# Best-32 attention: turned groups and the exponent's bias shared with VectorE, and a shorter exact path

## The reference, cut to what matters

```
scores = einsum('bthd,bghd->bhtg', Q, K) / sqrt(32)      # 2 batches, 4 heads, 256 x 4096
topv, topi = lax.top_k(scores, 32)
probs = softmax(topv)                                    # zero for all other keys
attn_mean = attn.mean(axis=heads)
c_t = einsum('btg,bgd->btd', attn_mean, x_vision) @ Wv
```

## Time and profile before

| what | value |
|---|---|
| median of three runs | 1144.29 us |
| the three runs | 1147.24, 1140.45, 1144.29 us |
| the profiled execution | 1140.79 us, its span 1139.5 us |
| busy in the span: TensorE | 955.4 us (84%) |
| VectorE | 848.7 us (74%) |
| ScalarE | 651.4 us (57%) |
| GpSimd | 295.7 us (26%) |

### The profile page before, as it was taken

The page is one execution under the profiler, slowest core; times in us unless marked ns, Lnnn a source line. Parts: engine busy times, 40 slices in busy tenths (PEclk is TensorE's granted clock), DMA queues, the critical chain, the costliest instruction groups (busy, mean ns, idle before and its releaser), DMA issues. The chain is left out here.

```text
span 1139.5 us, 20829 instructions
## 1 busy us (share of the span) xinstructions
PE 955.4 (84%) x7631; PEld 599.1 (53%) x7648; DVE 848.7 (74%) x1772; ACT 651.4 (57%) x1067; POOL 295.7 (26%) x313
## 2 busy tenths in 40 slices
PE   5997859999999999996989989248878888987586
PEld 5876724444444444443668875134555556634354
DVE  5775789999899999942567876998878785265447
ACT  3442307788788888874445425059999997202121
POOL 1000088899600000000112521006373631000010
PEclk9999958999999999997789996567799989997797
DMA  5867642222222222200312228002363136830000
GB/s 178 310 234 272 239 134 61 76 79 83 76 74 79 81 79 77 74 1 12 103 49 77 71 61 221 1 1 60 97 181 87 56 98 209 203 110 1 1 1 19
DMA packets 99322, 111.83 MB, mean 98 GB/s; under 512 B 26658, under 2 KB 75731, under 8 KB 99219
## 3 DMA queue, kind: packets, MB, share of 16 engines
q1 hardware_dynamic: 96802, 109.50, 32.0%
q10 hardware_dynamic: 2416, 0.99, 0.4%
HBM read 80.95 MB, written 29.43 MB: 97 GB/s over the span
## 5 line engine op out<-in xcount | busy, mean ns | idle before, releaser
L835 ACT ACTIVATE pT<-bank 128x512 f32<-128x512 f32 x512 | 278.5, 597 | 93.2 <-PE bank L752 71.9
L857 DVE TENSOR_REDUCE rmax<-bank 128x2 f32<-128x1024 f32 x256 | 307.3, 1223 | 26.4 <-PE bank L720 25.4
L764 PE MATMUL bank<-pT,V 128*17 128x256 f32 x2048 | 161.1, 387 | 4.7 <-ACT oT L841 4.5
L1679 PE MATMUL bank<-K1s,qs 97*128 97x512 f32 x256 | 116.7, 558 | 54.7 <-ACT below L1788 36.7
L752 PEld LDWEIGHTS bank<-qs,ks 49*128 49x128 f32 x1024 | 77.7, 186 | 112.4 <-ACT pT L835 98.9
L1943 POOL TENSOR_TENSOR total<-total,work 128x1024 f32<-128x1024 f32 x40 | 94.8, 2378 | 159.0 <-ACT work L1797 158.1
L752 PE MATMUL bank<-qs,ks 49*128 49x256 f32 x1024 | 130.0, 332 | 2.3 <-ACT pT L835 0.5
L720 PE MATMUL bank<-ks,qs 49*128 49x512 f32 x512 | 110.6, 427 | 16.2 <-DMA ks<-k_parts_d 9.0
L1679 PEld LDWEIGHTS bank<-K1s,qs 97*128 97x128 f32 x256 | 54.8, 227 | 69.8 <-ACT below L1788 38.0
L1849 DVE MAX8 cand<-work 128x8 f32<-128x128 f32 x384 | 76.4, 278 | 0.0
L764 PEld LDWEIGHTS bank<-pT,V 128*17 128x17 f32 x2048 | 34.5, 95 | 63.2 <-ACT pT L835 44.7
(11 more groups left out here) (452 smaller groups left out, 1841.6 us busy)
## 6 DMA issues: line engine op xcount, KB each, us to landing
k_parts_d<-kparts SPq DMA_DIRECT2D x48, 512.0 KB
ks<-k_parts_d SPq DMA_DIRECT2D x381, 64.0 KB, 2.2
K1s<-k_parts_d SPq DMA_DIRECT2D x96, 128.0 KB
cn<-in_ctx SPq DMA_DIRECT2D x32, 384.0 KB, 4.0
cx<-in_ctx SPq DMA_DIRECT2D x16, 384.0 KB, 5.0
w<-in_L_ffn_w SPq DMA_DIRECT2D x32, 128.0 KB, 2.7
w2e<-in_L_ffn_w SPq DMA_DIRECT2D x16, 128.0 KB, 2.4
W<-in_L_xattn_W SPq DMA_DIRECT2D x2, 1024.0 KB, 8.3
```

The costliest lines, as they stand in the source:

```text
L764: t = pe.matmul(bank[32 * c:32 * c + VW, 7, a * S:(a + 1) * S], V[:, b * NCH + 4 * g + c, h, :], pT[:, (at + 2 * (c // 2) + a) % 8, c % 2 ...
L835: p_made.up(act.activation(pT[:, at % 8, :], bank[:, 4 + at % 3, :], ACT.Exp))
L857: max_read.up(dve.tensor_reduce(rmax[p % 2][:, :, qt, c], bank[:, b0:b0 + 2, :], AX.X, ALU.max))
L1679: m = pe.matmul(bank[:, b0 + c, :], qs1[0:NROW1, b * H1 + h, q], K1s[h][0:NROW1, keys], start=True, stop=(what == "new"))
```

## The change

Four edits. (1) The copies of the turned parts with odd n of groups 0 and 1 are made by VectorE, at k = 2 of the step, after its candidates of that k. (2) `ebias` is made by VectorE, after the fourth piece of candidates and ahead of `rounds`. (3) The exact path leaves out its first MAX8, since `rounds` has found the best eight already, and its last pass; the tile then holds scores and -3e38. (4) So that one Relu serves both kinds of tiles, its scale is read from a tile `steep`: -2^66 without a flag, 1.0 with it, where the bias is 1e30.

```diff
-    NEX = 10
+    NEX = 9
-    LOW = -3e38
+    LOW, FAR = -3e38, 1e30
...
+    def by_vector(grp, n):
+        return grp < NGRP - 2 and n % 2 == 1
+
+    def copy_quad(copy, eng, grp, n):
+        at = NQ * grp + n
+        eng.wait_ge(*total_turned.at(at + 1))
+        if at >= 2:
+            eng.wait_ge(*c0_made.at(at - 1))
+        else:
+            eng.wait_ge(*K_stored.at(16 * 8))
+        aT_made.up(copy(xT[:, at % 2, :], bank[:, 6, :]))
...
-        def exp_bias(t):
-            j = t % 2
-            act.wait_ge(*lsum_made.at(t + 1))
-            ebias_made.up(act.activation(ebias[:, j:j + 1], lsum[:, j:j + 1], ACT.Identity, bias=ntop[:, j:j + 1], scale=-1.0))
...
             below_made.up(act.activation(below[:, part], home(t)[:, part], ACT.Relu, bias=steep_thr[:, t % 2:t % 2 + 1],
-                                         scale=-STEEP), n)
+                                         scale=steep[:, t % 2:t % 2 + 1]), n)
...
-                    if k == 3:
-                        exp_bias(s - 1)
...
-                if 4 * s + k in quads:
-                    copy_quad(*quads[4 * s + k])
+                if 4 * s + k in quads and not by_vector(*quads[4 * s + k]):
+                    copy_quad(act.copy, act, *quads[4 * s + k])
...
             with dve.If_ne(flagged, 0):
-                for k in range(KTOP // 8):
+                exact.up(dve.match_replace(home(t)[:, :], top[j][:, 0:8], home(t)[:, :], LOW))
+                for k in range(1, KTOP // 8):
                     take8(top[j][:, 8 * k:8 * k + 8], home(t)[:, :], home(t)[:, :], exact)
-                dve.wait_ge(*exact.at(NEX * t + 8))
-                exact.up(dve.tensor_scalar(home(t)[:, :], home(t)[:, :], LOW, -1e18, ALU.not_equal, ALU.mult))
-                exact.up(dve.memset(steep_thr[:, j:j + 1], 0.0))
+                exact.up(dve.memset(steep[:, j:j + 1], 1.0))
+                exact.up(dve.memset(steep_thr[:, j:j + 1], FAR))
             with dve.If_eq(flagged, 0):
+                dve.memset(steep[:, j:j + 1], -STEEP)
                 dve.tensor_scalar(steep_thr[:, j:j + 1], top[j][:, KTOP - 1:KTOP], STEEP, None, ALU.mult).then_inc(exact.sem, NEX)
...
+        def exp_bias(t):
+            j = t % 2
+            dve.wait_ge(*lsum_made.at(t + 1))
+            ebias_made.up(dve.tensor_tensor(ebias[:, j:j + 1], ntop[:, j:j + 1], lsum[:, j:j + 1], ALU.subtract))
...
                 if k == (s < NTL) and 1 <= s <= NTL:
                     over_to_sbuf(s - 1)
                     settle(s - 1)
+                if 4 * s + k in quads and by_vector(*quads[4 * s + k]):
+                    copy_quad(dve.tensor_copy, dve, *quads[4 * s + k])
+            if 1 <= s <= NTL:
+                exp_bias(s - 1)
             if s < NTL:
                 rounds(s)
```

More of the change, by code:

```diff
@@ L1542, in build @@
     over_i = [sb(f"over_i{j}", [1, 1], I32) for j in range(2)]
-    ntop, steep_thr = sb("ntop", [P, 2]), sb("steep_thr", [P, 2])
+    ntop, steep_thr, steep = (sb(n, [P, 2]) for n in ("ntop", "steep_thr", "steep"))
     etop = sb("etop", [P, KTOP])
@@ L1798, in exps @@
                                       ACT.Exp, bias=ebias[:, t % 2:t % 2 + 1]))
[L1800 to L1807, removed]
         act.preload_act_table_set("natural_log_exp_and_others")
@@ L1832, in best_scalar @@
                         log_sum(s - 1)
-                        exp_bias(s - 1)
                 if s < 3 and k == 3:
                     copy_kernel(s + 1, K_BANK)
-                if 4 * s + k in quads:
-                    copy_quad(*quads[4 * s + k])
+                if 4 * s + k in quads and not by_vector(*quads[4 * s + k]):
+                    copy_quad(act.copy, act, *quads[4 * s + k])
         exps(LAST, 3)
         for n in range(NQ):
-            copy_quad(NGRP - 1, n)
+            copy_quad(act.copy, act, NGRP - 1, n)
         for k, n in enumerate((P, DCM)):
```

## The result

The changed kernel is slower: 1153.59 us median of six runs (1150.29 to 1156.66) against 1140.81 (1138.56 to 1147.24), ratio 1.0104, 95% interval 1.0072 to 1.0136. The forecast was no change that can be measured; the time lies outside its range. The profiled execution took 1152.81 us with a span of 1151.5, 12.0 us more than the span before.

A forecast was written before the change was run, and what follows sets the result against it. ScalarE looked like the bound, VectorE nearly as tight; a new loop between them would cost 5.25 us against 6.65 gained in the exact path: net -1.4, 1141.8 us on the four-execution level, range 1131 to 1150.

The forecast's parts named there:

- the loop: Best-32 attention steps: VectorE's ebias waits for ScalarE's Ln, ScalarE's next mark_below for VectorE's settle; 13.65 us a period, loss 5.25 us.
- signal and the tensor_tensor of 128x1 that makes ebias: 0.18: VectorE, between ScalarE's Ln and `rounds`: signal plus making ebias takes 0.18 us per step, bounds 0.07 and 0.40.
- The exact path: First tile, VectorE: MAX8 (4.49 us) and comparison L1887 (2.24) removed, a memset (0.08) added; gain 6.65 us.
- ScalarE's losses and the copies: ScalarE sheds sixteen `exp_bias` of 0.36 us and eight copies of 0.47; on VectorE copies take 0.69 each, costing nothing.
- The pointer: ScalarE's `mark_below`: reading its scale from `steep` adds 0.09 us per instruction.
- mark_below to Ln: ScalarE, start of `mark_below` to end of Ln in each step: 4.35 us plus 0.09 for the scale read from `steep`.
- ScalarE doesn't stay the bound: Rival that ScalarE stays the bound in the steps, so its saved work counts: 12.8 us gained, 1130.4 us; chance 0.13.
- TensorE isn't late inside the loop: Rival that TensorE's cut matmuls at k = 2 come late at low clock: 0.8 us a step, 1149.8 us; chance 0.10.

## Why the prediction was wrong

**The step that failed** is a term of the loop: "signal and the tensor_tensor of 128x1 that makes ebias: 0.18", with the bounds 0.07 and 0.40. It was 1.43 us in nine steps of 2 to 14 and 2.33 in step 15. I took the price from small operations that read one tile as a tensor (ntop, 0.15 long) or run on another engine. The trace before has no tensor_tensor of VectorE beside a GpSimd add in this block (VectorE's own adds begin at 948.1, after GpSimd's last), and I took its silence for a small price. The upper bound should have been the add itself, 2.4 us: GpSimd runs 40 of them in these steps. 9 x 1.26 + 1.4 = 12.7 us is most of the 14.2 between the forecast's -1.4 and the measured +12.8; the 1.4 of step 15 rests on the run with the adds in quarters, and 1.26 on the steps with and without a held ebias.

"No row shows it" holds for this block only. The same trace of the kernel before shows the hold in the block ahead of it, and it stood in the groups that I read the price of a copy from:

```profile
L1357 DVE TENSOR_TENSOR hidp<-hid,hidp 128x512 fp32r<-128x512 f32 x16 | 22.0, 1377 | 1.4 <-ACT hidp L1308 1.4
L1353 DVE TENSOR_TENSOR hid<-bank,gate 128x512 f32<-128x512 f32 x16 | 11.1, 693 | 7.9 <-ACT gate L1302 7.8
```

Both are tensor_tensors of 128x512. The first has both inputs in SBUF, the second has one in a bank, and the first lasts twice as long on average. VectorE's timeline and then GpSimd's show why:

```profile
609.82 0.69 DVE L1357 TENSOR_TENSOR hidp<-hid,hidp 128x512 fp32r<-128x512 f32 x1 [0.69 <-ACT hidp L1308]
...
613.42 1.61 DVE L1357 TENSOR_TENSOR hidp<-hid,hidp 128x512 fp32r<-128x512 f32 x1
```

```profile
586.55 0.72 POOL L965 TENSOR_TENSOR w2p<-w2e,w2p 128x256 fp32r<-128x256 f32 x1
613.19 1.29 POOL L963 TENSOR_TENSOR w13p<-w,w13p 128x512 fp32r<-128x512 f32 x1 [25.92 <-ACT w13p L957]
614.43 1.20 POOL L965 TENSOR_TENSOR w2p<-w2e,w2p 128x256 fp32r<-128x256 f32 x1
```

Four of the sixteen L1357 run while GpSimd does nothing and last 0.68 to 0.69 us; the twelve that meet a running L963 last 1.60 to 1.61. The GpSimd instruction behind it is late in its turn: 1.20 us beside the held one, 0.72 alone. A tensor_tensor with one input in a bank is not held. Near the end of the trace two of four run wholly beside a GpSimd instruction of 2.3 us, and all four last 1.76; one of each kind, and the GpSimd instruction:

```profile
1102.79 1.76 DVE L2362 TENSOR_TENSOR sR<-bank,rmask 128x1536 f32<-128x1536 f32 x1 [5.66 <-PE bank L2245]
...
1108.50 1.76 DVE L2362 TENSOR_TENSOR sR<-bank,rmask 128x1536 f32<-128x1536 f32 x1 [1.06 <-PE bank L2245]
```

```profile
1102.56 2.34 POOL L2210 TENSOR_TENSOR gnw<-gr,gnv 128x1024 f32<-128x1024 f32 x1 [89.35 <-ACT gr L2311]
```

So it is not the tensor_tensor as such that is held, but the one with both inputs in SBUF.

The Trainium skill has the rule, which I didn't weigh. GPSIMD Engine Reference, section Specifications, says that GpSimd's SBUF interfaces are shared with VectorE and contend with VectorE instructions that have two SBUF inputs; VectorE: DVE Perf Modes, section Two Vector instructions with no wait between them, names the second read interface as the shared one. This case agrees: two inputs 1.43 us, one input and a pointer 0.21, at the same place. The runs show how long the hold lasts: until the running GpSimd instruction ends.

**The exact path**: right in kind, 6.23 us for 6.65. The first branch into it took 0.47 us longer after the flag was read (1.20 idle against 0.73).

**ScalarE's losses and the copies**: right. The eight copies cost VectorE nothing: its wait for the Ln is 0.82 us in steps with a copy and 1.42 in those without. Once the loop is open they gain something, 3.9 us by the medians and 2.1 in the steps of the traces.

**The pointer**: 0.10 us per mark, forecast 0.09. The operand isn't free.

**The loop**: right, and the larger insight of the two. Its period without the held ebias is 13.46 us, forecast 13.65 (its loss over steps 2 to 14 is 3.8 us in the run with the tensor_scalar, forecast 5.25); mark_below to Ln 4.40 for 4.44. With one instruction's form changed the kernel came out at -0.2%, forecast -0.1%.

**The rivals**: ScalarE doesn't stay the bound. It wasn't the bound in all steps before either. I took step 8 for all steps with turned groups, but in five of the eight from step 6 to 13 ScalarE already waited 0.64 to 0.80 us for TensorE. TensorE isn't late inside the loop; its granted clock is 1.00 in step 8, where I had feared a fall. That rival ended on the right side for the wrong reason. It does describe the kernels without the loop, the one before among them: TensorE sets most steps with turned groups, at a granted clock of 0.88 in those of 13.6 us and 0.86 to 0.94 in the long ones before. Why the clock is lower there stays open.

**What stays open** too: 1.3 us from step 16 to the c0T copies and about 1 in steps 2 and 3, and why the run with ebias alone loses 5 us more than the sum.

## What to carry to other kernels

When a small operation moves to VectorE, ask two questions of its place: what does its wait hold up behind it (here the rounds, the settle, and so the next tile), and what is GpSimd doing at that moment. A tensor_tensor with both inputs in SBUF can stand for the whole length of a GpSimd instruction; the same sum as a tensor_scalar with a pointer doesn't. A term that no row of the block shows should be looked for in the rest of the trace, by its operation and by what runs beside it. If no row shows it there either, it needs the longest thing it could wait for as its upper bound, not the dearest operation of its size.

## What the runs showed of the hardware that was not expected

VectorE's two-input operation on 128x1 values was held 1.27 us beyond its 0.16 by a GpSimd add of 2.35 us, and got in between two GpSimd adds that followed each other without a gap. MAX8, MATCH_REPLACE8, and the tensor_scalar ran beside the same adds at their usual lengths (16 MAX8 in 3.18 us with or without). GpSimd's adds weren't slowed by them: 2378 ns on average before and after. A longer two-input operation does slow GpSimd: beside the 128x512 of L1357 its 128x256 instruction took 1.20 us, and 0.72 alone. With one of the inputs in a bank, a VectorE tensor_tensor of 128x1536 took 1.76 us with and without GpSimd beside it.
